# Turns of the identity in TensorE's waits ahead of a stage's products, and a routed stage with both queries first and the gate last

## The reference

```python
x = L0_attn_x                                                # (2, 512, 512)
x = x + 0.5 * _L0_ffn_ref(_layernorm(x), ...)                # 4-bit weights, silu(a) * b, hidden 1376
x = x + _L0_attn_ref(_layernorm(x), ...)                     # state space ("mamba"): 128 heads of 64, state 128
x = x + 0.5 * _L0_ffn_ref(_layernorm(x), ...)                # the same weights again
x = x + 0.5 * _L1_ffn_ref(_layernorm(x), ...)                # routed: top 8 of 128 slots, a gate per token
x = x + _L1_attn_ref(_layernorm(x), ...)                     # attention: 32 heads of 16, 8 for keys and values
x = x + 0.5 * _L1_ffn_ref(_layernorm(x), ...)
```

```python
query = h @ Wq.T
router_scores = (query @ Wr.T) @ (aux_keys @ Wr.T).T / sqrt(48) + log_rel
top_idx = top_k(router_scores, 8)
w = softmax(over the 8 picked of (query . aux_keys / 8 + log_rel))
aux_out = (w @ aux_values[picked]) @ Wvd.T @ Wvu.T
u = clip(norm_var * 0.5 + sigmoid(gelu(h @ Wu1.T + bu1) @ Wu2.T + bu2) * 2.5, 0, 5)
gate = sigmoid(gate_w1 * clip((u - 0.5) / 1.5, 0, 1) + gate_bias)      # 0 where under 0.05
out = h + gate * aux_out
```

## Time and profile before

| | |
|---|---|
| median of three runs | 2520.4 us |
| the profiled execution's own time | 2520.89 us |
| its span, first to last instruction | 2519.0 us |
| mean granted TensorE clock in it | 0.973 |
| busy share: TensorE, VectorE, ScalarE, GpSimd | 94%, 66%, 52%, 53% |

### The profile page before, as it was taken

How to read it: one execution, slowest core, us unless ns; L and a number is a source line. 1 busy time by engine, 2 the same in 40 slices (tenths; PEclk the granted TensorE clock), 3 DMA queues, 4 the chain that set the end, 5 groups by cost and what they waited for, 6 DMA issues and landing times. The chain is left out here.

```text
span 2519.0 us, 32506 instructions
## 1 busy us (share of the span) xinstructions
PE 2371.8 (94%) x12122; PEld 1833.6 (73%) x12122; DVE 1661.3 (66%) x2163; ACT 1313.1 (52%) x1902; POOL 1329.8 (53%) x875
## 2 busy tenths in 40 slices
PE   6997899999999999999999999999889986989986
PEld 5876688888888888888888888888668753565643
DVE  5555887687588588588578678678365535674424
ACT  2323576477477467467467567567423223325533
POOL 2221498599499499589579679669622200000000
PEclk9998999999999999999999999999889998989997
DMA  4321333233233233233233323323134202000001
GB/s 128 97 80 46 115 110 105 89 96 119 79 111 115 80 104 103 93 100 114 88 102 109 92 89 117 98 95 102 46 84 97 90 14 78 1 2 2 2 1 47
DMA packets 163260, 203.98 MB, mean 81 GB/s; under 512 B 24380, under 2 KB 86080, under 8 KB 162976
## 3 DMA queue, kind: packets, MB, share of 16 engines
q1 hardware_dynamic: 163104, 201.90, 26.3%
HBM read 198.37 MB, written 3.15 MB: 80 GB/s over the span
## 5 line engine op out<-in xcount | busy, mean ns | idle before, releaser
L1892 POOL TENSOR_TENSOR mamba_w_lo<-mamba_raw,mamba_w_hi 128x512 fp32r<-128x512 f32 x272 | 436.1, 1613 | 289.9 <-ACT mamba_w_hi L1720 289.9
L76 PE MATMUL psum<-mamba_hT_lo,mamba_w_hi 128*128 128x512 f32 x1152 | 461.7, 401 | 5.6 <-DVE mamba_bc L1983 3.0
L77 PE MATMUL psum<-mamba_hT_hi,mamba_w_hi 128*128 128x512 f32 x1152 | 456.2, 396 | 0.0
L78 PE MATMUL psum<-mamba_hT_hi,mamba_w_lo 128*128 128x512 f32 x1152 | 456.1, 396 | 0.0
L1911 POOL TENSOR_SCALAR mamba_L<-mamba_A,mamba_ts 128x256 f32<-128x256 f32 (+1 forms) x256 | 334.3, 1320 | 0.1
L2015 DVE TENSOR_TENSOR mamba_L<-mamba_L,mamba_cb 128x1536 f32<-128x1536 f32 x128 | 302.0, 2359 | 22.2 <-ACT mamba_L L1769 16.5
L76 PEld LDWEIGHTS psum<-mamba_hT_lo,mamba_w_hi 128*128 128x128 f32 x1152 | 217.0, 188 | 55.9 <-DVE mamba_bc L1983 3.3
L1983 DVE SCALAR_TENSOR_TENSOR mamba_hid<-psum,mamba_cw,mamba_hid 128x1022 f32<-128x1022 f32 (+2 forms) x192 | 245.1, 1277 | 18.0 <-ACT mamba_hid L1727 13.5
L78 PEld LDWEIGHTS psum<-mamba_hT_hi,mamba_w_lo 128*128 128x128 f32 x1152 | 216.9, 188 | 52.4
L77 PEld LDWEIGHTS psum<-mamba_hT_hi,mamba_w_hi 128*128 128x128 f32 x1152 | 216.9, 188 | 49.1
L2042 DVE SCALAR_TENSOR_TENSOR mamba_zs_lo<-mamba_z,mamba_dgn,mamba_zs_hi 128x512 fp32r<-128x512 f32 x128 | 117.6, 923 | 172.0 <-ACT mamba_zs_hi L1792 172.0
(11 more groups left out here) (278 smaller groups left out, 5002.7 us busy)
## 6 DMA issues: line engine op xcount, KB each, us to landing
mamba_A<-mamba_a_dram SPq DMA_DIRECT2D x128, 512.0 KB, 4.4
mamba_raw<-in_win SPq DMA_DIRECT2D x144, 256.0 KB, 2.6
mamba_raw<-in_wout SPq DMA_DIRECT2D x128, 256.0 KB, 2.6
mamba_Eb<-mamba_e_dram SPq DMA_DIRECT2D x128, 128.0 KB, 3.0
ffn_raw<-in_w SPq DMA_DIRECT2D x80, 128.0 KB, 3.5
ffn_scl<-in_s SPq DMA_DIRECT2D x80, 128.0 KB, 3.7
ffn_scl<-in_s SPq DMA_DIRECT2D x86, 64.0 KB, 2.3
ffn_raw<-in_w SPq DMA_DIRECT2D x20, 256.0 KB, 2.6
```

The source lines that it names most:

```text
L76: e.matmul(out, wh, ml, start=start, stop=False)
L77: e.matmul(out, wh, mh, start=False, stop=False)
L78: return e.matmul(out, wl, mh, start=False, stop=stop)
L1892: e.tensor_tensor(w.lo[:, k % NSPLIT, :], raw[:, k % NRAW, :], w.hi_read[:, k % NSPLIT, :], ALU.subtract).then_inc(s["w_lo"], 1)
```

## The change

A helper `keep_clock(e, out, ident, n)` issues `n` transposes of the identity into a PSUM bank whose contents nobody reads. TensorE gets such turns

- at the start of all six stages: 14 at once, 6 after the first `var_ready`, and 4 after the second (mamba 6 after each, attention's norm only the first);
- in `q4_ffn` after `turn(0)` (4) and after each of the four `hT_lo` (4 each), ahead of `product(0, 0, 0)`;
- in `mamba` after each of the first four `hT_hi` (4 each), between the two `turn_rows`;
- in `attention` 8 ahead of the projections;
- in `routed_ffn` one ahead of each of the eight products of the gate, and 10 ahead of each `turn_weights`.

In `q4_ffn` VectorE does `low_rows` of tiles 0 and 1 ahead of `dequantize(0)`, and ScalarE does `high_rows(0)` ahead of `split(0)`. In `routed_ffn` TensorE does `query(1)` and `score(1)` ahead of the gate's products, ScalarE's two exponentials of the gate come after `exponentials(0)` and `exponentials(1)`, and VectorE does both `pick` ahead of the gate's chains.

```diff
--- before.py
+++ after.py
@@ -76,6 +76,12 @@
     e.matmul(out, wh, ml, start=start, stop=False)
     e.matmul(out, wh, mh, start=False, stop=False)
     return e.matmul(out, wl, mh, start=False, stop=stop)
+
+
+def keep_clock(e, out, ident, n):
+
+    for _ in range(n):
+        e.transpose(out[:, 0:P], ident[:], ident[:])
 
 
 class Chain:
@@ -213,6 +219,9 @@
 
             @block.tensor
             def _(e):
+                keep_clock(e, ps[2], ident, 14)
+                e.wait_ge(var_ready, 1)
+                keep_clock(e, ps[2], ident, 6)
                 for t in range(NT):
                     e.wait_ge(xr_ready if rms_w is not None else xn_ready, t + 1)
                     if t >= 2:
@@ -327,8 +336,8 @@
                         e.tensor_scalar(xn[:, t % HALF_T, :], x[:, t, :], mv[:, t, 0:1], rstd[:, t:t + 1],
                                         ALU.subtract, ALU.mult).then_inc(xn_ready, 1)
 
-                def low_rows(h):
-                    for t in range(h * HALF_T, (h + 1) * HALF_T):
+                def low_rows(h, first=0, end=HALF_T):
+                    for t in range(h * HALF_T + first, h * HALF_T + end):
                         sl = (slice(None), slice(None), slice(t * P, (t + 1) * P))
                         e.wait_ge(hT_hi, t + 1)
                         e.tensor_tensor(hT.lo[sl], ps[turned(t)].rearrange("p (a n) -> p a n", a=DT),
@@ -354,9 +363,10 @@
                 statistics(0)
                 statistics(1)
                 normalise(0)
+                low_rows(0, 0, 2)
                 e.wait_ge(sh_in, 16)
                 dequantize(0)
-                low_rows(0)
+                low_rows(0, 2, 4)
                 dequantize(1)
                 normalise(1)
                 low_rows(1)
@@ -410,8 +420,8 @@
                         e.copy(hT.hi[:, :, t * P:(t + 1) * P], ps[turned(t)].rearrange("p (a n) -> p a n", a=DT)
                                ).then_inc(hT_hi, 1)
 
+                high_rows(0)
                 split(0)
-                high_rows(0)
                 split(1)
                 high_rows(1)
                 split(2)
@@ -457,8 +467,16 @@
                                        a == 0, a == DT - 1)
                     last.then_inc((a_done, b_done)[m], 1)
 
+                keep_clock(e, ps[3], ident, 14)
+                e.wait_ge(var_ready, 1)
+                keep_clock(e, ps[3], ident, 6)
+                e.wait_ge(var_ready, 2)
+                keep_clock(e, ps[3], ident, 4)
                 turn(0)
-                e.wait_ge(hT_lo, HALF_T)
+                keep_clock(e, ps[3], ident, 4)
+                for t in range(HALF_T):
+                    e.wait_ge(hT_lo, t + 1)
+                    keep_clock(e, ps[3], ident, 4)
                 product(0, 0, 0)
                 turn(1)
                 product(0, 1, 0)
@@ -613,6 +631,11 @@
                     e.matmul(ps[OUT[t % len(OUT)]], wT[:, t * P:(t + 1) * P], vv[:], start=True, stop=True
                              ).then_inc(o_mm, 1)
 
+                keep_clock(e, ps[5], ident, 14)
+                e.wait_ge(var_ready, 1)
+                keep_clock(e, ps[5], ident, 6)
+                e.wait_ge(var_ready, 2)
+                keep_clock(e, ps[5], ident, 4)
                 for t in range(NT):
                     turn(t)
                 e.wait_ge(w_in, NL)
@@ -639,18 +662,21 @@
                 e.wait_ge(g_sb, 1)
                 e.wait_ge(vv_sb, 1)
                 score(0)
+                query(1)
+                score(1)
                 e.wait_ge(gelu, 2)
                 e.wait_ge(lv_used, 1)
                 for t in range(NT):
+                    keep_clock(e, ps[3], ident, 1)
                     last = e.matmul(ps[2][:, t:t + 1], u3[:, t * P:(t + 1) * P], sc[:, 1:2], start=True, stop=True)
                 last.then_inc(lr_mm, 1)
-                query(1)
-                score(1)
                 e.wait_ge(u_sb, 2)
+                keep_clock(e, ps[3], ident, 10)
                 turn_weights(0)
                 for t in range(NH_T):
                     value(t)
                 e.wait_ge(z1, 1)
+                keep_clock(e, ps[6], ident, 10)
                 turn_weights(1)
                 for t in range(NH_T, NT):
                     value(t)
@@ -714,18 +740,18 @@
                 tanh(1)
                 take_query(0)
                 take_scores(0)
-                e.wait_ge(z1, 1)
-                e.activation(s1[:], s1[:], ACT.Exp, scale=-1.0).then_inc(ez1, 1)
                 e.wait_ge(affine, 2)
                 residual(0)
-                e.wait_ge(z2, 1)
-                e.activation(gate[:], gate[:], ACT.Exp, scale=-1.0).then_inc(ez2, 1)
                 take_query(1)
                 take_scores(1)
                 exponentials(0)
+                e.wait_ge(z1, 1)
+                e.activation(s1[:], s1[:], ACT.Exp, scale=-1.0).then_inc(ez1, 1)
                 take_weights(0)
                 residual(1)
                 exponentials(1)
+                e.wait_ge(z2, 1)
+                e.activation(gate[:], gate[:], ACT.Exp, scale=-1.0).then_inc(ez2, 1)
                 take_weights(1)
 
             @block.vector
@@ -804,8 +830,10 @@
                 e.wait_ge(lv_used, 1)
                 ch.link(e.reciprocal(lvs[:], lvs[:]))
                 ch.step(e.tensor_scalar(s2[:], lv[:], lvs[:], 0.5, ALU.mult, ALU.mult))
+                pick(0)
                 e.wait_ge(lr_mm, 1)
                 e.tensor_scalar(s1[:], ps[2][:, 0:NT], 0.5, sc2[:, 0:1], ALU.mult, ALU.add).then_inc(z1, 1)
+                pick(1)
                 e.wait_ge(ez1, 1)
                 ch.link(e.tensor_scalar(s1[:], s1[:], 1.0, None, ALU.add))
                 ch.link(e.reciprocal(s1[:], s1[:]))
@@ -814,13 +842,11 @@
                 ch.link(e.tensor_scalar(s1[:], s1[:], -0.5, 1.0 / 1.5, ALU.add, ALU.mult))
                 ch.link(e.tensor_scalar(s1[:], s1[:], 0.0, 1.0, ALU.max, ALU.min))
                 e.tensor_scalar(gate[:], s1[:], sc2[:, 1:2], sc2[:, 2:3], ALU.mult, ALU.add).then_inc(z2, 1)
-                pick(0)
                 e.wait_ge(ez2, 1)
                 ch.link(e.tensor_scalar(gate[:], gate[:], 1.0, None, ALU.add))
                 ch.link(e.reciprocal(gate[:], gate[:]))
                 ch.link(e.tensor_scalar(msk[:], gate[:], 0.05, 0.5, ALU.is_ge, ALU.mult))
                 ch.link(e.tensor_tensor(gate[:], gate[:], msk[:], ALU.mult))
-                pick(1)
                 factor(0)
                 add(0)
                 factor(1)
@@ -1086,6 +1112,7 @@
                     last.then_inc(out_mm, 1)
                     spare[0] = (x_done, s + 1)
 
+                keep_clock(e, ps[7], ident, 8)
                 e.wait_ge(w_in, 7 * 16)
                 for b in range(SEQS):
                     for i in range(NV):
@@ -1656,7 +1683,14 @@
                         last = e.transpose(ps[6][:, t * P:(t + 1) * P], dec[:, q:q + P], ident[:])
                     last.then_inc(s["ts_turned"], 1)
 
+                keep_clock(e, ps[7], ident, 14)
+                for h in range(2):
+                    e.wait_ge(s["var_ready"], h + 1)
+                    keep_clock(e, ps[7], ident, 6)
                 turn_rows(0)
+                for a in range(DT):
+                    e.wait_ge(s["hT_hi"], a + 1)
+                    keep_clock(e, ps[3], ident, 4)
                 turn_rows(1)
                 e.wait_ge(s["dw_lo"], 1)
                 time_step(0)
```

## The result

| | before | change |
|---|---|---|
| median (lowest to highest, runs) | 2519.51 us (2518.23 to 2521.07, 7) | 2509.89 us (2503.08 to 2512.39, 7) |
| ratio, 95% interval | | 0.9957 (0.9944 to 0.9969) |
| span of the profiled execution | 2519.0 us | 2501.3 us |
| mean granted clock in it | 0.973 | 0.987 |

The change is faster by 9.6 us by the two medians, twice the 4.8 us that were forecast. The ratio goes by all the runs and not by the medians alone; it says 10.8 us (7.8 to 14.1).

What follows compares the result with a forecast made beforehand. TensorE, busy 94% of the span, was taken as the bound, partly at half clock. Terms -2.45 - 2.2 - 1.05 + 0.4 - 1.0 + 1.0 = -5.3 took 2520.9 to 2515.6 us; range 2509.5 to 2521.5.

Steps and rivals of the forecast that it cites:

- the tails' term: Ends of both routed stages: new order gives +0.5 us in the first, -1.5 in the second, sum -1.0.
- ffn: Both ffn stages: 0.6 us paid for turns, first product then at full clock; -2.45 and -2.2 us.
- mamba and the routed starts: Mamba -1.05 us, mainly from a faster `turn_rows(1)`; turns at the two routed starts cost +0.4 in all.
- Attention: Eight turns ahead of the first projection, in no wait, cost +1.0 us.
- The first two bursts bring nothing: Each stage's start: clock still falls, so turns before the second `var_ready` gain nothing by themselves and cost nothing.
- (1): Rival: clock held through the wait at the stages' starts; -16.5 us, 2504 us; chance 0.08.
- (2): Rival: routed tail loses the clock behind thin products; +3 us a stage, 2521 to 2522 us; chance 0.12.
- (3): Rival: turns do not lift the clock and are pure cost in all stages; +10.7 us, 2531 us; chance 0.04.

Runs made afterwards that it cites:

- e6: The kernel before with only the turns and new order of the two ffn stages: 2514.57 us, ratio 0.9982.
- e11: The change once more, unchanged, for a second profile: 2508.25 us, ratio 0.9958.
- e3: The change without the 14 and 6 turns ahead of the second `var_ready` (mamba keeps 6 behind the second): 2512.68 us, ratio 0.9970.
- e12: The kernel before once more, unchanged, for a second profile: 2518.84 us.
- e10: The kernel before with only the turns of mamba and of the two routed starts, every order as before: 2518.45 us, ratio 0.9996.
- e9: The kernel before with attention's turns alone (14 and 6 in the norm, 8 ahead of the projections): 2520.93 us, ratio 1.0005.
- e5: The kernel before with only the routed stage's new order, no turns, ffn untouched: 2512.47 us, ratio 0.9973.
- e8: e7 with longer bursts in the statistics, 24 and 20 turns for 14 and 6 (attention's norm 40 and 12): 2504.90 us, ratio 0.9939.
- e7: The change without the 8 turns ahead of attention's projections and without the turns in the routed tail: 2506.01 us, ratio 0.9955.
- e2: The change with all its turns but every order as in the kernel before: 2511.11 us, ratio 0.9968.

## Why the prediction was half the size

The direction was right, and the time lies at the very low end of the range (2509.5). The step that failed is the tails' term: -1.0 us was forecast, and the routed order alone measured -6.8. By the steps of the forecast:

- **ffn, right in size, in part by luck.** Forecast -2.45 and -2.2, in all -4.65; e6 measured -4.5 (-6.8 to -2.3). In the second stage the first product starts 13.5 us after the stage's begin, before 12.8: 0.7 paid, 0.6 forecast. In the first it comes at 23.39 us in e11 and 23.31 in e3, 23.4 forecast, and at 22.18 in the change's profile and in e6, where the clock was up earlier. There the first turns did what the forecast gave them no credit for, so e6's 4.5 us hold something that my 4.65 did not. The forecast also put the stage's 14 turns at 1.7 us, at full clock; in the first stage they ran at half clock (20 in 4.65 us). And the 6.1 us of slow products that I wanted to give back by half are not typical: in e12 the first products ran at full clock.
- **mamba and the routed starts, not contradicted.** Forecast -1.05 and +0.4, in all -0.65; e10 measured -1.0 (-3.0 to +1.3), which can't tell it from nothing. `turn_rows(1)` takes 2.02 us, 1.94 forecast.
- **Attention, not contradicted.** Forecast +1.0; e9 measured +1.3 (-0.8 to +3.5). In the traces the turns cost 0.8. In e11 they ran at half clock and took 1.6 us; half of that came back in the products behind them, of which the first eight took 4.4 us, 5.2 before.
- **The tails, wrong: the mis-sized term.** Forecast -1.0 for both. e5, the order without its turns, measured -6.8 (-9.3 to -4.3). The forecast gave 24.2 us from the end of `score(0)` to the end of the last add; the change's trace has 22.3 (2066.04 to 2088.33). Three things, the first two for the change's own tail, the third for what it is compared with:
  1. The eight adds. I took 3.27 us for four from the earlier trace rows. That row says `[1.26 <-PE psum L613]`: the adds went at the pace at which TensorE delivered. The very step in which I said that VectorE becomes the bound used a duration that TensorE had set. One add takes 0.75 us there and 0.74 in the change's trace; what differs is how soon the next one follows. Four adds back to back take 2.73, so two sets end 1.1 us sooner.
  2. The way to the first add. Forecast 17.4 us behind `score(0)`, measured 16.5. I charged the eight turns between the gate's products at 1.0 us; the block took 2.26 with them and 1.84 without (e5), so they cost 0.4. The remaining 0.3 to 0.5 is spread over the rest of the chain of nine steps; no single one stands out.
  3. The kernel before. It had lost the clock behind the gate's products in one stage of the profile that I read, and loses it in both in e12 and in eight of the ten stages with that order. I took the lucky stage as the rule for the first tail. At 25.7 us in place of 23.7 the first stage's gain grows by 2.0.

  So the sum is (22.3 - 23.7) + (22.3 - 25.7) = -4.8 against the profiled execution and -6.8 against e12, where -1.0 stood. These 3.8 to 5.8 us are nearly all of the 6 us by which the ratio's gain of 10.8 passes the forecast's 4.8. The turns in the tail were no part of it: e5's first tail, without them, is 0.9 us shorter still (21.4), its second 0.1 (22.2).
- **"The first two bursts bring nothing", wrong in a part of the executions.** e3 against the change says some 3 us, just not resolved; the two profiles of the change show one start held and one not.

Of the rivals: (1), the clock held through the wait, is true of the first routed start in the change's first profile and of all starts behind the first ffn stage in e8, attention's norm apart. Its time, 2504, is what e8 reached (2504.9), but not for its reason alone: the tails give 5 to 7 us of it, so the held clock is worth less than I priced it. (2), the tail loses the clock, did not happen in the change: the first four `value` take 3.70 us in all four routed stages of its two profiles. Without the turns it happens: in e5 they take 5.35 and 6.32 us. It costs nothing that shows in the first stage and 0.8 us in the second, not the 3 I had priced, for the adds wait mostly for the gate's chain and not for TensorE; I had granted the adds half of the cover, and they give more. (3), turns don't count, is refuted: at 1847.2 us the clock rose on transposes alone. By the Trainium skill, page "TensorE: Matmul & The Clock Gate", Part 4, it wouldn't have; the trace disagrees here as it did before.

What stays open: what decides, for the same instructions, whether the clock falls (change against e11); how much of the routed order's gain comes from each of the three engines whose order it moves; and whether the denser turns of e8 gain more than the 1 to 4 us that its times say against e7's.

## What to carry to other kernels

Before using a row's duration for an operation that becomes the bound, look at its bracket and its count: a row of several instructions that waits on another engine's products tells the pace of that engine, and the same instructions back to back may be a sixth shorter (2.73 against 3.27 us). Try moving thin products (one column each) behind the dense work of others, where a lower clock finds something to hide under: here the order that did this, and that also moved ScalarE's exponentials and VectorE's picks, brought 6.8 us, and regaining the clock in both ffn stages 4.5. If a wait ahead of dense work is filled to keep the clock, try filling most of it (in e8's profile the clock then held, and its gain over e7 isn't settled), and put nothing on the path: the eight turns in attention cost 0.8 us, those in the routed tail some 0.4 a stage.

## What the runs showed of the hardware

The granted clock was not a function of the instructions alone: the same program had 1.00 through 2037 to 2047 us in one execution and 0.50 from 2046.1 in another, with 1.88 us of work in the first 3.3 us of both. Attention's length differed by 7 us between executions of one code (349.0 and 356.1), and by 3 in the kernel before (355.6 and 352.5). A single profile can't tell a gain of that size from chance; 8 to 11 runs of each part could put it within some 2 us. And a TensorE that the profile shows as busy can lose its clock: the sixteen matmuls of the gate have one column each, their block is 1.84 us of unbroken work, and behind it `query(1)` took 5.34 us in three of four routed stages of the kernel before (and 5.2 to 6.4 in eight of ten stages of all kernels with that order), but 3.65 in both of e2's, where a turn stood ahead of each product.
